# Combining and linear attention: GpSimd's second answer ahead of two gathers, the first offset and the sums ahead of the second offset, the magnitudes ahead of normalising

## What is computed

```
h = h + layernorm(x + moe_out) * gamma + beta      # x = layernorm(h); moe_out: two rows times two gates
x = layernorm(h)
q, k, v = split(x @ w_qkv.T)                       # 12 heads of 16
q = q / max(sum_n |q|, eps);  k = k / max(sum_n |k|, eps)
kv = einsum('bhnd,bhne->bhde', k, v)
out = einsum('bhnd,bhde->bhne', q, kv)
h = h + out @ w_proj.T + b_proj
```

## Time and profile before

| what | value |
|---|---|
| median of 3 runs | 2828.34 us (2826.10 to 2831.12) |
| the profiled execution | 2826.7 us, its span 2824.4 us |
| TensorE, share of the span busy | 85% |
| VectorE | 71% |
| ScalarE | 52% |
| GpSimd | 35% |
| mean granted TensorE clock | 0.881 |

### The profile page before, as it was taken

The page is one execution under the profiler, slowest core; times in us unless marked ns, Lnnn a source line. Parts: engine busy times, 40 slices in busy tenths (PEclk is TensorE's granted clock), DMA queues, the critical chain, the costliest instruction groups (busy, mean ns, idle before and its releaser), DMA issues. The chain is left out here.

```text
span 2824.4 us, 45185 instructions
## 1 busy us (share of the span) xinstructions
PE 2386.8 (85%) x14046; PEld 1708.7 (60%) x14047; DVE 2005.1 (71%) x5460; ACT 1480.2 (52%) x2580; POOL 997.9 (35%) x1024
## 2 busy tenths in 40 slices
PE   8999999999996999999965999926678785776666
PEld 4444444444445788888854999925577674444444
DVE  6777777777745788888853444447697867999996
ACT  2444444444443667676643565536565641666665
POOL 1100100100000355555552444468776720434333
PEclk9999999999997999999977999967787896667766
DMA  2000000000002011111116777721111100000000
GB/s 56 0 18 13 0 18 13 0 9 1 0 1 86 27 47 47 47 46 50 43 59 205 257 256 256 254 90 50 48 45 42 47 10 22 21 25 25 21 25 25
DMA packets 69332, 162.66 MB, mean 58 GB/s; under 512 B 13009, under 2 KB 32662, under 8 KB 68894
## 3 DMA queue, kind: packets, MB, share of 16 engines
q1 hardware_dynamic: 39618, 94.16, 10.2%
q0 software_dynamic: 21504, 44.99, 5.5%
q10 hardware_dynamic: 8064, 21.68, 2.5%
HBM read 63.87 MB, written 63.88 MB: 45 GB/s over the span
## 5 line engine op out<-in xcount | busy, mean ns | idle before, releaser
L418 DVE TENSOR_REDUCE pmax<-ppre 112x1 f32<-112x512 f32 x656 | 424.5, 686 | 161.8 <-PE ppre L260 161.8
L211 ACT ACTIVATE prob<-pscore 128x896 f32<-128x896 f32 x336 | 308.0, 917 | 423.0 <-PE pscore L293 423.0
L307 PE MATMUL pout<-prob,xkey 128*64 128x448 f32 x1344 | 327.8, 566 | 0.4 <-ACT prob L211 0.4
L718 POOL DMA_INDIRECT rows_in<-xr,idx x224 | 233.8, 1044 | 238.3 <-DVE idx L1189 179.8
L260 PE MATMUL ppre<-xh,yh 49*112 49x512 f32 x656 | 291.2, 446 | 7.8 <-DVE pmax L418 4.1
L260 PEld LDWEIGHTS ppre<-xh,yh 49*112 49x112 f32 x656 | 112.6, 172 | 239.3 <-issue 103.5
L1631 POOL DMA_INDIRECT yg<-rows_out,place x224 | 234.2, 1046 | 62.4 <-issue 62.1
L193 POOL CAST yh<-ynext 113x448 fp32r<-113x448 f32 x28 | 17.2, 614 | 667.3 <-DVE pmax L418 639.2
L293 PE MATMUL pscore<-yh,xh 49*128 49x448 f32 x700 | 241.0, 421 | 0.4 <-DVE yh L438 0.4
L2146 POOL TENSOR_TENSOR yg<-y,gout 112x512 f32<-112x512 f32 x112 | 141.1, 1270 | 275.5 <-DVE y L2370 275.5
L1481 POOL TENSOR_TENSOR zl<-z,zh 128x448 fp32r<-128x448 f32 x126 | 144.5, 1147 | 220.0 <-ACT zh L1447 210.5
(11 more groups left out here) (366 smaller groups left out, 6460.4 us busy)
## 6 DMA issues: line engine op xcount, KB each, us to landing
wd<-down SPq DMA_DIRECT2D x63, 512.0 KB, 3.0
xb<-rows_in SPq DMA_DIRECT2D x63, 448.0 KB, 3.6
rows_out<-yb ACTq DMA_DIRECT2D x63, 336.0 KB, 3.2
out<-ho SPq DMA_DIRECT2D x28, 336.0 KB, 2.8
rows_in<-zero SPq DMA_DIRECT2D x15, 448.0 KB
rows_in<-xr,idx POOLq DMA_INDIRECT x224
yg<-rows_out,place POOLq DMA_INDIRECT x224
xkey<-in_xkey SPq DMA_DIRECT2D x4, 800.0 KB, 6.5
```

The lines of the kernel that those rows point to most:

```text
L211: nc.scalar.activation(prob[j % 3][:, :, :], pscore[j % 2][:, :, 0:CH], ACT.Exp).then_inc(exped, 1)
L307: mm = pe.matmul(pout[i * LO:(i + 1) * LO, 0:CH], xkey[b % 2][:, 2 * j + i, :], prob[j % 3][:, i, :], start=(j == 0), stop=(i == 1 and j = ...
L418: nc.vector.reduce_max(pmax[:, q, 2 * block + half:2 * block + half + 1], bank(u, depth), AX.X).then_inc(pre_max, 1)
L718: nc.gpsimd.indirect_dma_start(rows_in, bass.IndirectOffsetOnAxis(ap=idx[r % G3][:, 2 * q + k:2 * q + k + 1], axis=0), xr[r % G3][:, q, :] ...
```

## The change

GpSimd computes the second answer (`factor4`) ahead of the last two gathers of the step. VectorE takes the sums ahead of the second offset; the first offset, of the chunk for the next step, is made between them, at the end of the step before instead of after `low`. ScalarE takes the first magnitudes and the copies ahead of normalising. No instruction is added or removed.

```diff
                     factor(s + 3)
+                if here(s + 2):
+                    factor4(s + 2)
                 if here(s + 4):
                     gather_rows(s + 4, (3,))
-                if here(s + 2):
-                    factor4(s + 2)
...
                     rows_normed(s + 2)
+                if s >= 0:
+                    magnitudes(s, c, 0)
+                    copies(s)
                 if here(s + 1):
                     normalise(s + 1)
-                if s >= 0:
-                    copies(s)
-                    magnitudes(s, c, 0)
...
-                if here(s + 2):
-                    offset(s + 2)
                 if here(s + 3):
                     add_experts(s + 3)
...
                     add_out(s - LATE)
-                if here(s + 2):
-                    offset4(s + 2)
                 if s >= 0:
                     dve.wait_ge(S["qk_mm"], 3 * s + 2)
                     nc.vector.tensor_reduce(sums[b % 2][:, 1, c:c + 1], pqk[1][:, 0:CH], AX.X, ALU.add,
                                             apply_absolute_value=True).then_inc(S["b_sum"], 1)
+                if here(s + 3):
+                    offset(s + 3)
+                if here(s + 2):
+                    offset4(s + 2)
```

## The result

The changed kernel takes 2850.86 us (median of 4 runs, 2847.16 to 2852.55) against 2828.55 for the kernel before in the same rounds: a ratio of 1.0082, 95% interval 1.0069 to 1.0094, so 22.3 us slower. Its profiled execution took 2851.13 us.

The account below looks back on a forecast made before the run. GpSimd bounds plain steps before, a 14.20 us round through the gathers after. Stretch terms sum to +15.0 us on the profiled 2826.7, giving 2841.7; the median lies 1.6 higher, so 2843 us, range 2831 to 2854.

Parts of the forecast that it names:

- (a): GpSimd's second answer ahead of two gathers: a round of 14.20 us a step wherever chunks are still gathered.
- (b): VectorE's first offset and sums ahead of the second offset: worth nothing in plain steps, -4.8 us at the first image change.
- rival 3: Gathers land later, 2.2 us after the issue: round 14.75, +8 us more, 2851 us in total; chance 0.08.
- step 9: Third step of an image, TensorE at half clock: the step lasts 18.1 us instead of 14.25.
- the tail: Last steps, behind A(24): late magnitudes in step 26 move the split of step 27 to 2312.3; +2.3 us.
- Rival 2: Gathers arrive in time and GpSimd binds at about 13.25 us a step: about -10 us, 2818; chance 0.07.
- A(6) to A(9): First image change, between ends of the second norm's statistics in steps 6 and 9: -4.8 us through earlier sums.
- (c): ScalarE's magnitudes ahead of normalising: 7.9 us from product to next split, hidden in plain steps, not where TensorE is late.
- step 16: Third step of an image, like the one after A(9): the step lasts 17.7 us.
- step 23: Third step of an image: TensorE had its clock back sooner, so the step stays under 14.2 us.
- Rival 1: TensorE keeps its full clock, ScalarE's order never bites before A(24): sum +5.6 us, 2834; chance 0.20.
- rival 4: TensorE binds plain steps: four of eight with outputs at half clock give +15 us more, 2857; chance 0.10.

Follow-up runs that it names:

- (a) alone: Only GpSimd's second answer moved ahead of the last two gathers, against the kernel before: 2836.79 us, ratio 1.0049.
- (a)+(b): GpSimd's and VectorE's new orders together, ScalarE as before, against the kernel before: 2826.19 us, ratio 1.0007.
- (b) alone: Only VectorE's sums and next first offset moved ahead of the second offset, against the kernel before: 2811.70 us, ratio 0.9955.
- (b) once more: The kernel with only VectorE's new order, run again with more rounds against the kernel before: 2808.59 us, ratio 0.9947.
- (c) alone: Only ScalarE's first magnitudes and copies moved ahead of normalising, against the kernel before: 2880.13 us, ratio 1.0195.

## Why the prediction was right, and where it was not

The direction came out, and so did the round of (a) and the gain of (b), by the mechanisms named. The size did not: 2850.9 is 8 us above the forecast of 2843, outside the 5 us around it that were given 0.55, and the touched phase grew by 28.3 us where the sum had 15.0. Only 8 of these 13 show in the total because the profiled execution reached the phase 3.6 us earlier than the one before, and because 1.6 us had been added for the median, which this time lies next to the profiled execution. The time is also the 2851 of rival 3, whose mechanism did not come. And the nearly right sum of the first seven stretches owes something to luck (step 9 below). One step failed, the tail was mis-sized, and one step was left unmade.

- *(a), the round of 14.20.* Right: 14.15 to 14.33 in most plain steps, from power to combining mostly 4.07 to 4.27 (4.08 taken), landing mostly 1.65 to 1.86. With (a) alone and with (a)+(b) the same. Rival 2 falls, and rival 3 as a rule for every step. The estimate of 2.2 us that the prediction takes from the Trainium skill, "DMA: Bandwidth & Descriptors", section "Anatomy of one DMA — SWDGE (gpsimd) path", is above most landings here; three were longer, 2.39 (step 9), 2.50 (step 11) and 2.90 (step 20). VectorE's wait ahead of combining was 36.2 us in 19 steps, not some 1.3 in 15, and its L1928 did not come to wait for nothing: 22.4 us in 14.
- *(b), -4.8 in A(6) to A(9) and nothing elsewhere.* Right inside the whole change (-5.6). Alone it is worth 13 to 15 us, because without (a) GpSimd bounds plain steps and its first power becomes 0.5 us shorter. The prediction saw that power and priced its shortening at nothing, rightly, since (a)'s round hid it.
- *(c), step 16.* Right in mechanism, 1.2 us short: the magnitudes came 0.3 us after A(16), and the step took 18.87 and not 17.7. Of this, 0.9 is VectorE waiting for the two gathers that stand behind the second power, which stands behind normalising.
- *(c), step 9.* Wrong, and the nearly right sum is luck. TensorE had a clock of 0.93 from 2040.48 to 2046.32 us, and the magnitudes of step 9 came 4.3 us ahead of A(9), so (c) cost nothing there: the step took 15.0, not 18.1, and what it has over 14.2 is the late landing. But step 11 took 16.46: there the last two gathers lie 2.7 us apart instead of 1.3, with 1.70 idle on "issue", which is not explained, and land late. The term of +5.9 measured +5.2; (a)+(b), without (c), has 58.42 us in the same stretch, +3.6.
- *(c), step 23: the step that failed.* "Step 23 had the clock back sooner and stays under 14.2." Before, from 2264.49 to 2271.67, and after, from 2272.97 to 2283.29, the granted clock while TensorE worked towards that product was

```profile
2264.49:2271.67 7.18, 7.02 (x39) 6.53 (x38) 7.03 (x21) 5.68 (x14) 1.40 (x3) 0.91 0.05 14
```

```profile
2272.97:2283.29 10.32, 10.32 (x35) 9.95 (x35) 10.04 (x30) 1.73 (x5) 4.69 (x5) 0.50 0.10 26
```

  0.91 before and 0.50, the lower of the two levels, after. The product came late, and the step cost 18.8 instead of 14.2: 4.7 us of the miss. The clock of before was carried over to the changed kernel, and it is not even fixed for one kernel. The same stretch of step 23, from the end of the cast to the first magnitudes, in (b) alone and in (b) once more:

```profile
2246.50:2256.19 9.69, 9.69 (x35) 9.43 (x35) 9.41 (x26) 5.67 (x15) 3.46 (x3) 0.55 0.03 10
```

```profile
2250.24:2256.42 6.18, 6.18 (x35) 6.10 (x35) 6.00 (x19) 5.68 (x14) 0.72 (x2) 0.88 0.08 19
```

  0.55 and 0.88 in two executions of one kernel; in step 16 it is the other way round, 0.86 and 0.61. So whether a step has the higher clock could not be read from one profile. What makes the low clock dear is (c). Before, the magnitudes of step 9 came 0.21 us after A(9) at 0.50, and the step took 14.25. With (b) and one gather behind the second answer (its L1854 and L1711 are L1852 and L1709 here), and ScalarE's old order:

```profile
2251.28:2261.63 10.35, 10.35 (x35) 9.98 (x35) 10.03 (x30) 5.68 (x15) 4.58 (x5) 0.50 0.07 20
```

```profile
2261.63 0.54 ACT L1854 ACTIVATE junk<-pqk 128x448 f32<-128x448 f32 x1 [4.67 <-PE pqk L1711]
```

  A(23) is 2261.33 there, so the magnitudes come 0.30 us after it, exactly as late as in the changed kernel, and the step takes 14.25 us, not 18.83: normalising was done while ScalarE waited for TensorE.
- *The tail, +2.3.* Mis-sized: +10.3. The magnitudes of step 26 come 20.9 us after A(24) instead of 18.4, and the split 6.7 us behind them instead of 3.7. After it the block of maps and outputs, which had no term, runs at a clock of 0.84, 0.92 before, with its first 9.6 us at 0.54: +4.9. With ScalarE's old order from step 24 on both are gone (22.25 and 45.16 us).
- *Left out: the power behind normalising.* The prediction followed normalising's delay forward to the transposes and the cast, but not back to GpSimd, which may not overwrite the factors. In the whole change (b) hides most of it, and (a) keeps a rest of 24.9 us of waits in 7 steps. With (c) alone it costs 25 us.
- *Rival 1*, full clock, was refuted in steps 16 and 23 and held in step 9; *rival 4* did not show: plain steps stayed at 14.2.

What stays open is what makes the clock fall where it does. Over all the kernels it lay between 0.50 and 0.91 in that part of step 23; no run changed TensorE's work alone, and most kernels were profiled once.

The version worth keeping is (b) alone, about 0.5% faster than before.

## What to carry to other kernels

Before an instruction is moved later on a queue, list who waits for it in both directions: those who read its result, and those who may not overwrite what it reads; a 112x4 buffer in one copy tied four engines into one ring here. A reordering of three engines is three changes whose prices don't add (+12, -13 and +55 gave +22), so each is worth a run alone, and here the gain lay in the one that filled a wait with work that waited for nothing. A round that goes through a transfer is measured from the issue to the consumer: moving one of two gathers behind an answer was free, moving both cost 0.2 us a step where GpSimd's powers were long and 0.7 where (b) had made its round shorter. A granted clock read in one execution is a sample: an order that is only good while the clock is high in one particular step should be priced for both levels.

## What the runs showed of the hardware

- GpSimd's power on 112x4 takes 1.04 us, and 1.64 when it starts during a VectorE addition of two 112x768 tiles of SBUF (some at image changes take 1.75 to 3.0, which nothing here explains). The order of VectorE's work set the mean of six between 1144 ns and 1649 ns, and with it the step.
- An indirect gather waited for by VectorE is usable 1.65 to 1.86 us after its issue instruction ends in most steps, when it is the last of two, and 2.39 to 2.90 in three; the issue pitch is 1.24 us when nothing stretches it.
- The granted clock of TensorE over the same products of step 23 was 0.91 before and 0.50 in the changed kernel, and 0.55 and 0.88 in two executions of one kernel, (b) alone.
